# The second mixture's front (norms, transposes and logits of its first tiles) moved into the last eight turns of the second attention

## The reference, cut to what matters

```python
    x = x + jnp.tanh(g_xattn[1]) * _L1_xattn_ref(ctx_1024, ctx_1024, _layernorm(x, axis=-1), mask_Bx1xSxS2_ik1, L1_xattn_Wv, L1_xattn_Wk, L1_xattn_Wq)
    x = x + jnp.tanh(g_ffn[1]) * _L1_ffn_ref(_layernorm(x, axis=-1), L1_ffn_proj, L1_ffn_C1, L1_ffn_Win1, L1_ffn_Wout1, L1_ffn_C2, L1_ffn_Win2, L1_ffn_Wout2)

    def _L1_ffn_ref(x, proj, C1, Win1, Wout1, C2, Win2, Wout2):
        a = entmax15(layernorm_noaffine(jnp.einsum('btd,de->bte', x, proj)))
        g1 = jnp.einsum('bte,er->btr', a, C1)
        h = cp_mumoe(x, g1, Win1, Wout1)
        h = jax.nn.gelu(h, approximate=False)
        g2 = jnp.einsum('bte,er->btr', a, C2)
        return cp_mumoe(h, g2, Win2, Wout2)
```

## Time and profile before

| | us |
|---|---|
| three timed runs | 1123.71, 1111.95, 1123.23 |
| their median | 1123.23 |
| the profiled execution | 1111.36 |
| its span, first to last instruction | 1109.3 |
| around the span | 2.1 |
| busy in the span: PE, DVE, ACT, POOL | 996.6, 743.5, 492.7, 417.5 |

### The profile page before, as it was taken

How to read it: one execution, slowest core, us unless ns; L and a number is a source line. 1 busy time by engine, 2 the same in 40 slices (tenths; PEclk the granted TensorE clock), 3 DMA queues, 4 the chain that set the end, 5 groups by cost and what they waited for, 6 DMA issues and landing times.

```text
span 1109.3 us, 17730 instructions
## 1 busy us (share of the span) xinstructions
PE 996.6 (90%) x6273; PEld 604.7 (55%) x6273; DVE 743.5 (67%) x2239; ACT 492.7 (44%) x957; POOL 417.5 (38%) x575
## 2 busy tenths in 40 slices
PE   9999999997999988998899999999999993599970
PEld 6356666665444444346766666666445452277750
DVE  2757999998776768856766656556687877344334
ACT  2656666664344433652233333332444441265534
POOL 0072344444421735032442312001427656166670
PEclk7999999998999989999999999999999996799995
DMA  8069000000000030000024333343001011511116
GB/s 197 6 232 283 1 1 1 1 2 20 1 2 1 1 122 1 0 1 1 1 59 97 77 78 79 78 90 64 1 4 36 30 33 45 207 32 36 38 44 233
DMA packets 37847, 62.00 MB, mean 56 GB/s; under 512 B 6049, under 2 KB 22152, under 8 KB 36994
## 3 DMA queue, kind: packets, MB, share of 16 engines
q1 hardware_dynamic: 33154, 52.40, 17.4%
q0 software_dynamic: 4608, 8.50, 2.3%
HBM read 40.47 MB, written 21.45 MB: 56 GB/s over the span
## 4 chain that ended last, share of the span: by engine, by line
PE 70%; DVE 17%; DMA 4%; ACT 4%; issue 3%; POOL 1%; SPq 0%; DVEq 0%; POOLq 0%; ACTq 0%
PE bank L1183 8%; PE bank L1245 6%; PE bank L483 5%; PE bank L627 5%; PE bank L1199 5%; PE bank L526 5%; PE bank L1256 3%; PE bank L693 3%; PE bank L427 3%; PE bank L512 2%; PE bank L519 2%; DVE nmax L2215 2%; ACT att L1458 2%; DMA big_a<-gates 1%; PE bank L646 1%
## 5 line engine op out<-in xcount | busy, mean ns | idle before, releaser
L1183 PE MATMUL bank<-big_b 128*128 128x512 f32 x288 | 135.8, 596 | 0.0
L1750 POOL TENSOR_SCALAR xn<-xw,mean,rstd 128x128 f32<-128x128 f32 x62 | 49.1, 801 | 180.2 <-DVEq L2782 90.8
L2215 DVE TENSOR_REDUCE nmax<-bank 128x16 f32<-128x1024 f32 x64 | 77.9, 1218 | 46.5 <-PE bank L633 28.1
L1647 ACT ACTIVATE att<-bank 128x512 f32<-128x512 f32 (+1 forms) x72 | 43.0, 597 | 134.7 <-PE bank L1183 132.3
L1972 POOL DMA_INDIRECT expert_outs<-big_a,big_b x80 | 77.7, 972 | 57.6 <-DVE big_a L2856 34.5
L1199 PEld LDWEIGHTS bank<-big_b,att 128*128 128x128 f32 (+1 forms) x576 | 72.9, 191 | 32.1 <-issue 19.9
L2718 DVE TENSOR_TENSOR att<-att,bank 128x512 f32<-128x512 f32 (+1 forms) x72 | 49.2, 684 | 57.5 <-PE bank L1199 54.7
L1963 POOL DMA_INDIRECT expert_rows<-xw,big_b x64 | 63.6, 994 | 50.7 <-DVEq L2317 34.3
L1199 PE MATMUL bank<-big_b,att 128*128 128x128 f32 (+1 forms) x576 | 77.9, 278 | 3.9 <-DVE xw L2072 2.6
L1458 ACT ACTIVATE att<-bank 128x1024 f32<-128x1024 f32 x64 | 62.1, 1022 | 41.4 <-PE bank L669 41.4
L1245 PE MATMUL bank<-big_b 128*128 128x384 f32 (+1 forms) x192 | 74.5, 532 | 0.7 <-ACT big_b L1674 0.7
(11 more groups left out here) (446 smaller groups left out, 2157.2 us busy)
## 6 DMA issues: line engine op xcount, KB each, us to landing
big_a<-gates SPq DMA_DIRECT2D x14, 1024.0 KB, 9.7
expert_rows<-big_b SPq DMA_DIRECT2D x1, 5240.0 KB, 19.9
expert_outs<-big_b SPq DMA_DIRECT2D x1, 4096.0 KB, 31.9
big_a<-expert_outs SPq DMA_DIRECT2D x6, 512.0 KB, 8.2
big_a<-expert_rows SPq DMA_DIRECT2D x1, 2620.0 KB, 14.2
big_a<-in_mask SPq DMA_DIRECT2D x2, 1024.0 KB, 12.6
big_b<-in_w_in SPq DMA_DIRECT2D x1, 2048.0 KB, 8.1
out<-xw SPq DMA_DIRECT2D x8, 256.0 KB, 2.7
```

The source lines that it names most:

```text
L1183: mm = nc.tensor.matmul(bank[2 * (n % 3) + k][:, :], w13[:, k, c * 128:(c + 1) * 128], xnT_all[:, g * GW:(g + 1) * GW], start=True, stop=True)
L2215: nc.vector.tensor_reduce(nmax[:, j], psum[:, 2048:3072].rearrange("p (h t) -> p h t", t=T), AX.X, MAX, negate=True).then_inc(s.free, 1)
```

## The change

The logits of tiles 0 to 7 (groups 0 and 1) are made inside turns of the second attention. GpSimd computes the means and roots of tiles 0 to 3 and 4 to 7 (`moments_and_roots`) ahead of its norms of batches 8 and 12, and of tiles 8 to 23 after batch 15. Ahead of its norms of each of the batches 8 to 15 it normalises one tile for the mixture into one of four spare quarters of `xn` (`ahead`). TensorE transposes that tile beside the batch's two and multiplies the one before by `proj1` behind `maxima_transposes`; ScalarE copies both, each right behind a copy that it does anyway. `similarity_rows()` moves from behind batch 15 to ahead of GpSimd's norms of batch 4. In the mixture VectorE and ScalarE make no moments and roots; GpSimd makes those of tiles 24 to 31. Groups 3, 4 and 5 are normalised by ScalarE (`norms`, with `Identity`), 6 and 7 by GpSimd. `delta_roots(0)` stands behind the logits of group 5. The 24 multiplications of `warm_array` ahead of the mixture become 4.

```diff
@@ tensors and counts
+        ahead = [xn[:, k // 2, 2 + k % 2] for k in range(4)]
+        AHEAD, FA = 2 * TPG, 2
@@ TensorE, second attention
 def to_features(b):
                     for j in range(2):
                         mm = nc.tensor.transpose(dst[:, j * 128:(j + 1) * 128], xn[:, b % 2, j], ident[:, :])
+                    if b >= B - AHEAD and not wide:
+                        mm = nc.tensor.transpose(dst[:, 3 * 128:4 * 128], ahead[b % 4], ident[:, :])
 def maxima_transposes(b):
+                    if not wide and b + 1 >= B - AHEAD and b + 1 < B:
+                        t = b + 1 - (B - AHEAD)
+                        mm = nc.tensor.matmul(bank[6][:, 3 * 128:3 * 128 + E1], xnT_all[:, t * 128:(t + 1) * 128], proj1,
+                                              start=True, stop=True)
                     mm.then_inc(s.nmT, 1)
@@ TensorE, mixture
-                features(0)
-                features(1)
-                logits(0)
-                logits(1)
-                for g in range(2, NG - 1):
+                for g in range(FA, NG - 1):
                     features(g)
                     logits(g)
...
-            warm_array(24, 0)
+            warm_array(4, 0)
             pe.wait_ge(layer_done, 3)
@@ ScalarE, second attention
 def feature_evac(b):
+                    if b >= B - AHEAD and not wide:
+                        t = b - (B - AHEAD)
+                        cp = nc.scalar.copy(xnT_all[:, t * 128:(t + 1) * 128], bank[6][:, 3 * 128:4 * 128])
+                    cp.then_inc(s.xT_evac, 1)
 def maxima_evac(b):
+                    if not wide and b + 1 >= B - AHEAD and b + 1 < B:
+                        cp = nc.scalar.copy(lg[:, b + 1 - (B - AHEAD), 0:E1], bank[6][:, 3 * 128:3 * 128 + E1])
+                    cp.then_inc(s.nmT_evac, 1)
@@ ScalarE, mixture
+                def norms(g):
+                    act.wait_ge(front_sems.xT, max(g - FA - 1, 1))
+                    for j in range(TPG):
+                        t = TPG * g + j
+                        ins = nc.scalar.activation(xn[:, g % 2, j], x[:, t], ACT.Identity, bias=lnt[:, 2, t:t + 1],
+                                                   scale=rstd[:, t:t + 1])
+                    ins.then_inc(front_sems.xn, 1)
...
+                nc.scalar.activation(warm[:, 2:3], ones[0:1, 0:1], ACT.Sqrt)
+                act.wait_ge(r_xn, 1)
+                norms(FA + 1)
+                norms(FA + 2)
+                for g in range(FA, NG - 1):
                     feature_evac(g)
                     logit_evac(g)
-                    if g == 4:
+                    if g == FA + 1:
+                        norms(FA + 3)
+                    if g == FA + 3:
                         delta_roots(0)
@@ GpSimd, attention_norms
                     if n == 1 and 2 * b == 2 * TPG:
                         pool.wait_ge(stats_ready, 1)
+                    if n == 1 and b == 4:
+                        similarity_rows()
+                    if n == 1 and b in (B - AHEAD, B - AHEAD + TPG):
+                        first = b - (B - AHEAD)
+                        pool.wait_ge(s.split, first // 2 + 5)
+                        moments_and_roots(slice(first, first + TPG))
+                    if n == 1 and b >= B - AHEAD:
+                        if b - TPG >= B - AHEAD:
+                            pool.wait_ge(s.xT, b - TPG + 1)
+                        norm_ahead(b - (B - AHEAD), ahead[b % 4])
@@ GpSimd, order of the layers
             attention_norms(1, narrow)
-            similarity_rows()
+            pool.wait_ge(narrow.split, 15)
+            middle, shift = slice(2 * TPG, 6 * TPG), lnt[:, 2, 2 * TPG:6 * TPG]
+            moments_and_roots(middle)
+            step(nc.gpsimd.tensor_tensor(shift, mean[:, middle], rstd[:, middle], MUL))
+            step(nc.gpsimd.tensor_scalar(shift, shift, -1.0, None, MUL))
+            pool.wait_ge(narrow.xT, B)
+            for j in range(TPG):
+                ins = norm_ahead(2 * TPG + j, ahead[j])
+            ins.then_inc(r_xn, 1)
             pool.wait_ge(layer_done, 3)
@@ GpSimd, mixture
-                for g in range(3, NG - 1):
-                    norms(g)
+                moments_and_roots(slice(6 * TPG, NT))
+                norms(NG - 2)
                 squares(0)
                 gates(0)
                 norms(NG - 1)
@@ VectorE
                 def variances(self):
-                    dve.wait_ge(front_sems.lg_evac, 2 * self.count)
+                    if self.count == 1:
+                        dve.wait_ge(narrow.nmT_evac, B - 1)
+                    else:
+                        dve.wait_ge(front_sems.lg_evac, 2 * self.count - FA)
...
-                for g in range(3):
-                    norms(g)
...
-            ln_statistics(2)
```

More of the change, by code:

```diff
@@ L1441, in feature_evac @@
                     act.wait_ge(s.xT, t0 + b + 1)
[L1442 to L1443 removed]
+                    cp = nc.scalar.copy(xnT[:, (b if wide else b + 1) % 2, 0:S], bank[7 if wide and b < 2 else 6][:, 0:S])
+                    if b >= B - AHEAD and not wide:
+                        t = b - (B - AHEAD)
+                        cp = nc.scalar.copy(xnT_all[:, t * 128:(t + 1) * 128], bank[6][:, 3 * 128:4 * 128])
+                    cp.then_inc(s.xT_evac, 1)
                 def query_evac(b):
@@ L1733, in spread_keys, with similarity_rows @@
                                             head8[:, :].unsqueeze(2).broadcast_to([128, H // 2, T]), MUL).then_inc(g_built, 1)
+            def similarity_rows():
+                pool.wait_ge(m.rb_evac, 2)
+                for k in range(3):
+                    rows_k = slice(32 * k, 32 * k + 32)
+                    mid = nc.gpsimd.tensor_scalar(rb[rows_k], rb[rows_k], ident[rows_k, 32 * k:32 * k + 1], None, MUL)
+                    step(mid)
+                    for n in range(k + 1):
+                        step(nc.gpsimd.tensor_copy(rb3[rows_k], rb[rows_k]))
+                        if n < k:
+                            step(nc.gpsimd.tensor_tensor(rb[rows_k], rb[rows_k], rb3[rows_k], SUB))
+                pool.drain().then_inc(m.g2, 1)
             def attention_norms(n, s):
@@ L1791, in statistics0, with norm_ahead @@
                     step(tt(r, r, apart, MUL))
-                step(tt(square, mu, r, MUL))
-                ts(square, square, -1.0, None, MUL).then_inc(att_sems.ready, 1)
+            def statistics0(g):
+                tiles = slice(TPG * g, TPG * g + TPG)
+                shift = lnt[:, 2, tiles]
+                pool.wait_ge(att_sems.normed, 4 * g + 5)
+                moments_and_roots(tiles)
+                step(nc.gpsimd.tensor_tensor(shift, mean[:, tiles], rstd[:, tiles], MUL))
+                nc.gpsimd.tensor_scalar(shift, shift, -1.0, None, MUL).then_inc(att_sems.ready, 1)
+            def norm_ahead(t, dst):
+                return nc.gpsimd.tensor_scalar(dst, x[:, t], mean[:, t:t + 1], rstd[:, t:t + 1], SUB, MUL)
             def unscaled(g):
@@ L2512, in mumoe @@
             def mumoe():
-                def norms(g):
-                    if g > 1:
-                        dve.wait_ge(front_sems.xT, g - 1)
-                    for j in range(TPG):
-                        ins = norm(xn[:, g % 2, j], TPG * g + j)
-                    ins.then_inc(front_sems.xn, 1)
                 def rank1(g):
```

67 lines of the change are left out of this document (22 added, 45 removed).

## The result

| | before | changed kernel |
|---|---|---|
| timed runs | 11, 1111.75 to 1123.71 us | 11, 1126.2 to 1137.17 us |
| median | 1116.04 us | 1128.49 us |
| profiled execution, its span | 1111.36, 1109.3 us | 1128.49, 1126.7 us |
| granted clock, mean of the span | 0.951 | 0.941 |

A forecast was written before the change was run, and what follows sets the result against it. TensorE, hardly ever idle, bounds the second attention; a chain bounds the mixture's front. 15.9 + 2.7 + 2.1 - 1.4 - 2.0 = +17.3 us on the median 1123.23 gives 1140.5 us, range 1122.7 to 1147.4.

The forecast's parts named there:

- The stall: Second attention, turn 2: TensorE waits for batch 4 behind the moved similarity rows, 16.2 us, 15.9 net.
- the wait for the exponential: TensorE's idle 0.32 us ahead of `values` in a turn; over after the stall, so 15.9 us net.
- The clock behind it: After the stall in the second attention: 5.5 us at half clock, losing 2.7 us; bounds 1.0 and 5.
- The eight turns: Last eight turns of the second attention: added logit products cost 2.1 us, the added transpose nothing; bounds 1.0 and 2.5.
- The end of the attention: Turns 13 and 14: VectorE's split casts, no longer beside the rows, return to normal, -1.4 us.
- The front: From the attention's end to `rank1(0)`: shorter chain, partly at half clock, gains 2 us; bounds 0 and 5.5.
- The stall came: Against the first rival: no stall in turn 2, total -1.3 us, 1121.9 us, not slower; 6 in 100.
- not from 283.94: Second rival: the rows start at 283.94 without waiting for VectorE's roots, stall 5.9, total +5.4, 1128.6 us; 3 in 100.
- the third rival: Last eight turns: GpSimd's new work holds up VectorE's split, 6.2 us more, total +23.5, 1146.7 us; 5 in 100.
- The half clock did not last: Against the fourth rival: half clock a dozen us behind the stall and the whole front, +22.8, 1146.0 us; 6 in 100.
- The five terms: Whole kernel: stall 15.9, clock 2.7, eight turns 2.1, attention's end -1.4, front -2.0; sum +17.3 us.

The follow-up runs named there:

- e1: Kernel before with only similarity_rows() moved ahead of GpSimd's norms of batch 4; median 1132.17 against 1117.98 us, ratio 1.0128.
- e2: Changed kernel with similarity_rows() back behind batch 15; median 1121.6 against 1117.98 us for the kernel before, ratio 1.0027.
- e3: Changed kernel with the rows dealt out in six pairs ahead of norms of batches 4, 5, 6, 7, 10 and 11; median 1119.06 us, ratio to before 1.0004.
- e8: Changed kernel with six of the twelve row operations ahead of batch 4, the rest behind batch 15; ratio to the kernel before 1.0111.
- e4: Changed kernel with 68 unread multiplications on TensorE in turn 2, ahead of the transposes that wait; ratio to the kernel before 1.0142.
- e5: e3 plus 16 warming multiplications behind the first transposes of the mixture's front; ratio to the kernel before 0.9981 less not applicable: 0.9975.
- e6: e3 with ScalarE's square roots of the first quarter behind the logits of group 3 instead of group 5; ratio to the kernel before 0.9981.
- e9: Changed kernel with all twelve row operations ahead of both waits of batch 4 instead of behind them; ratio to the kernel before 1.0053.
- e10: e3 plus 16 front warming multiplications and early square roots, with row pairs moved behind norms of batches 3, 5, 7 and 8; ratio to before 1.0005.
- e11: Kernel before with 31 instead of 24 warming multiplications ahead of the mixture; ratio to the kernel before 0.9952.

## Why the prediction was right

**The stall.** TensorE's transposes are 16.0 us late, where the prediction had 16.2, or 15.9 less the wait for the exponential. e1 shows it with no other part of the change, e2 and e3 take it away, and e8 halves its cause and gets what sticks out. The arithmetic used three rows only: the end of VectorE's roots, the length of the rows, TensorE's need.

**The clock behind it.** 2.6 us at 2.7. The two terms share the small wait: in e4, at full clock and with the exponential long ready, the same work takes 4.58 us, 0.4 less than the 4.96 before. In the prediction's terms that makes a net stall of about 15.7 at 15.9 and a clock loss of 3.0 at 2.7, two small errors that cancel in the sum of 18.6. The half clock lasted until about 324.5, 6.4 us behind the first transposes, at 5.5 predicted.

**The eight turns.** 1.5 us (0.18 each) at 2.1: about 0.09 us of the 0.27 of product and loads was covered in a turn. The added transpose cost nothing, as predicted.

**The end of the attention.** -1.4 us as said: from the maxima of turn 3 on, 1.5 us of turns and -1.4 of casts leave +0.1, and that is the table's 18.7 to 18.8. In e1, which has only the -1.4, the attention from turn 2 on is 102.7 us, 1.5 shorter than in the changed kernel.

**The front.** -2.8 us at -2.0. The path was the predicted one: the thresholds ended 22.4 us behind the end of the attention (at 444.70), where the prediction's steps give 19.5 at full clock and 3.4 for the half clock, and `rank1(0)` followed 6.4 us later, at 6.5 predicted. ScalarE's norms were cheaper than the row of the first attention (3.2 us for eight instead of 3.9). What the half clock cost here was not measured by itself. In e3 it lasted some 17 us, to 427, and taking it away in e5 brought 6.7 us; by that rate the 10 us of the changed kernel are an estimated 4, at 3.4 predicted. One thing the prediction had not weighed: TensorE's chain of groups ends nearly as late as the path through the square roots, so that roots made early bring only 1.9 us (e6).

**The rivals.** The stall came, from 294.28 and not from 283.94. VectorE's cast of the split in the last eight turns stayed at 0.18 to 0.20 us (just ahead of them, at 346.29, one took 0.37 and no turn was longer for it), so the third rival is out for the small operations and norms of this change. The half clock did not last: 6.4 us behind the stall, and 10 of the front's 28.8. The Trainium skill, page "SBUF — State Buffer", section "Who interferes with whom", which spoke for the third rival, is borne out where GpSimd subtracts or casts (e3, e9, e10). It says that a VectorE instruction with two SBUF inputs waits for a GpSimd instruction that reads SBUF; beside GpSimd's scaling of the rows this case's trace agrees only in part (below).

**What the sum did not have, and luck.** The five terms, as measured up to `rank1(0)`, add up to 15.9 us and not to 17.3. That the spans lie 17.4 apart is in part luck. Between the first and the eighth maximum of the third attention the changed kernel loses 1.6 us, and all experiments lose more there: 60.7 to 70.4 us at clocks of 0.92 to 0.77, where the profile of before has 59.1 at 0.94. The order of the program there is the same in all. Since these are single profiles, and of before the one that took 1111.36 where its median was 1116.04, I can't say how much of it is chance. It fits that the medians' difference, 12.4 us, is smaller than the profiles' 17.1, and that e2, e3 and e10, with marks of -4.1 to +1.9 us up to `rank1(0)`, all measure within 0.3% of before. Kernels with a short front tend to a long third attention (22.8 beside 64.7 to 69.7; 31.3 to 31.7 beside 59.1 to 63.8). Whether one causes the other stays open; no kernel here kept the clock up in the third attention.

## What to carry to other kernels

Work that "nobody waits for" has a price as soon as it stands ahead of something in the same queue: subtract the time of need from the end of the moved block, and add what the clock costs behind it (here 3.0 us behind an idle piece of 16, and 1.3 behind one of 5). Before moving work out of a chain, see at which clock the chain runs: seven multiplications more in the old kernel (e11) gave a ratio that the intervals cannot tell from the best that was reached with the moved front (0.9952 and 0.9935). When placing GpSimd work with large two-input or casting operations, look at all of VectorE's small operations, not only at the one that was seen to suffer.

## What the runs showed of the hardware

GpSimd's subtraction and cast of 32x1024 held up a VectorE operation that began beside them until they ended: the subtraction for 2.10 and 1.99 us instead of 0.17 and 0.15 (e9, e10), the cast for 1.07 us instead of 0.19 (e3). A maximum that VectorE took from a PSUM bank beside both (302.97 in e9) had its usual 1.22 us. GpSimd's scaling (TENSOR_SCALAR, 2.84 us) did so only in part. In e9 it ran from 297.12 to 299.98: VectorE's operation of 297.30 ended at 298.28, and the next seven, all with two inputs from SBUF, took 0.18 us each (the scaling, and the first and last of the seven):

```profile
297.12 2.86 POOL L1756 TENSOR_SCALAR big_a<-big_a,ident 32x1024 f32<-32x1024 f32 x1
...
298.31 0.18 DVE L2105 SCALAR_TENSOR_TENSOR rstd<-lnt,rstd 128x20 f32<-128x20 f32 x1
...
299.59 0.18 DVE L2105 SCALAR_TENSOR_TENSOR rstd<-lnt,rstd 128x20 f32<-128x20 f32 x1
```

In the changed kernel a cast of 298.51 beside the scaling of 298.31 ended at 299.45:

```profile
298.31 2.83 POOL L1756 TENSOR_SCALAR big_a<-big_a,ident 32x1024 f32<-32x1024 f32 x1
298.51 0.94 DVE L2263 CAST msplit<-nmax 128x32 bf16<-128x32 f32 x1
...
300.78 0.39 DVE L2096 TENSOR_SCALAR lnt<-lnt 128x4 f32<-128x4 f32 x1
```

So some 1.15 us from its start the scaling let VectorE through, both times. The profiles hold 14 such cases (casts, TENSOR_SCALARs and the operation of e9, begun 0.12 to 0.80 us into a scaling), and all ended 1.12 to 1.16 us from its start. That also fits turn 12 of the kernel before, which the prediction could not explain: its cast of 371.28 began 1.68 us into the scaling of 369.60 and took 0.18 us. It is not free from there on for every operation: VectorE's TENSOR_SCALAR of 300.78, 2.47 us into the scaling, took 0.39 us instead of 0.17 and ended with it (301.17 and 301.14). Why, no run here tells.
